# A of tile 0 behind the first weights on SyncE's queue, A of tile 1 on ScalarE's, the gathers' index made by VectorE

## The chip, the core and the metric

The kernel runs on one core of one Trainium2 chip. The metric is the device time of one execution in microseconds (us), as the median of several runs. Profiled executions come from the chip's profiler; all times inside them count from the start of the span.

The engines are TensorE (PE; its weight loads are listed apart as PEld), VectorE (DVE), ScalarE (ACT), GpSimd (POOL) and SyncE (SP, which here only issues DMAs). Each engine works through its own list of instructions in order and waits on semaphores where the program says so. ACT and POOL issue DMAs too, besides their arithmetic.

## What is computed

64 sequences of 32 rows and 512 columns pass through two residual layers. In each, a sequence picks its own weights by an index:

```python
def reference(x, itok_B_0_15, itok_B_0_23, L0_cond_weights, W, b, lora_As, lora_Bs):
    x = x + jnp.einsum('bct,bcd->bdt', x, L0_cond_weights[itok_B_0_15])
    base_out = jnp.einsum('bti,oi->bto', x, W) + b
    h = jnp.einsum('bti,bir->btr', x, lora_As[itok_B_0_23])
    lora_out = jnp.einsum('btr,bro->bto', h, lora_Bs[itok_B_0_23])
    return x + base_out + lora_out * 2.0
```

x is 64x32x512 in float32, W is 512x512, a lora_A is 512x16, a lora_B is 16x512.

## The kernel before

**Tiles.** Four sequences make one tile of 128 rows, so there are 16 tiles (u = 0 to 15). The two layers are swapped where that is possible: z = x (I + W) + x A B is made first, and the small mixing matrix of layer 0 is put on z afterwards (`mix`). For a tile the main product runs over four chunks k of 128 input columns. The host lays out x transposed.

**Precision.** Tiles 1 to 15 use split products: each operand is cut into a rounded part (ACT writes x_hi, wa) and a rest (DVE writes x_lo and the rest part of wa), and three fast products are summed (`products`, L548). The wide buffer wa holds W plus identity beside the A matrices. Tile 0 alone is computed in plain float32, straight from the loaded data: its main product is `first_chunk` (L619), its product with A is L626, its product with B is L580 (`lora(0, half)`).

**The start.** Host data for the start lie in one tensor `first`, which SP loads in five pieces (`load_first`, L209): piece 0 is half of x of tile 0 with W chunk 0, piece 1 the other half with W chunk 1, piece 2 is W chunk 2, piece 3 is W chunk 3, and piece 4 (`PIECE_OF_X1`) is x of tile 1. ACT first issues the two small loads of indices (L313, L314), then, after it has read four adapter numbers from the first of them, the four loads of A of tile 0 (L323, 32 KB each, 256 bytes to a partition). SP, after its five pieces, reads adapter numbers too and issues four loads of A of tile 1 (`load_a(1)`, L224), then x of tile 2 (L214), the weights of layer 0 (L237), A of tile 2 and so on.

**The steps around the change.** In program order:

- DVE adds the identity to the diagonal block of each W chunk (`add_identity`, L445) and makes the rest of each W chunk (`rest_w`, L449), then the two halves of the rest of x of tile 1 (`rest_x1`, L434), then the rests of A of tile 1 (`rest_a`, L455).
- ACT rounds W chunks 0 to 2 (`round_w`, L353), rounds the first half of x of tile 1 (`round_x1(0)`, L343), copies A of tile 0 into its place for the product (L388), rounds the second half of x of tile 1, A of tile 1 (L363) and W chunk 3.
- PE runs nine warm-up products on zeros (L541), `first_chunk` for k = 0 to 3, which needs piece k and for one half of its columns the added identity, then L626 with A of tile 0 (waits for `a0_ready`), then the main product of tile 1 (L548), whose first step waits for W chunk 0, for the first half of x of tile 1 and for the first half of A of tile 1, rests included. After four of its eight steps come the two halves of L580, which wait for the first gather of B and for the masked product of L626.
- POOL makes the identity and masks, then the row index for all gathers of B (L274, L276, from ids_p_sb), and then for each tile copies one column of the index (`gather_b`, L289) and issues an indirect DMA (L291). Three gathers are issued ahead.

Afterwards the loop over tiles 1 to 14 runs with loads three tiles ahead.

Of the kernel before, what the change touches and what calls it, by code (L numbers as in the profile page):

```python
# [10 lines left out]
ALU = mybir.AluOpType  # L11
# [5 lines left out]
def lora_residual_program(nc, first, xt, ids_row, ids_of_p, w0, bias, lora_a, lora_b, out):  # L17
# [5 lines left out]
    _, _, KC, _ = xt.shape  # L23
    O = out.shape[2]
    TILES = xt.shape[0] + 2
    C, S0, _ = w0.shape
    SLOTS, _, _, R = lora_a.shape
    T = KC * P
    J = P // C
# [6 lines left out]
    NA = 3  # L36
# [7 lines left out]
    PIECE_OF_X1 = 4  # L44
    DIAGONAL_HALF = tuple(k * P // HALF for k in range(KC))
    HJ = J // 2
# [12 lines left out]
    with ExitStack() as ctx:  # L59
# [143 lines left out]
        @block.sync  # L203
        def _(sp):
            adapters = [sp.alloc_register(f"adapter{j}") for j in range(J)]

            def load_first(n):
                at = slice(PIECES[n], PIECES[n + 1])
                sp.dma_start(first_sb[:, at], first[:, at]).then_inc(first_loaded[n], 16)  # L209

            def load_x(u):
                if u >= 2 + NX:
                    sp.wait_ge(x_ready, u - NX + 1)
                sp.dma_start(x_raw[(u - 2) % NX][:, :, :], xt[u - 2]).then_inc(x_loaded[(u - 2) % NX], 16)  # L214

            def load_a(u):
                if u == NA:
                    sp.wait_ge(a0_ready, 1)
                elif u > NA:
                    sp.wait_ge(a_ready, 2 * (u - NA))  # L220
                sp.load(adapters, ids_sb[0:1, u * J:(u + 1) * J])
                for j in range(J):
                    slot = sp.snap(adapters[j], min_val=0, max_val=SLOTS - 1)
                    sp.dma_start(a_raw[u % NA][:, j:j + 1, :, :].rearrange("p j k r -> p j (k r)"),  # L224
                                 lora_a[bass.ds(slot, 1)].rearrange("s p k r -> p s (k r)")
                                 ).then_inc(a1_half_loaded[j // HJ] if u == 1 else a_loaded[u % NA], 16)

            def store_y(u):
                sp.wait_ge(y_ready, u + 1)
                sp.dma_start(out_rows[u * P:(u + 1) * P, :], y_sb[u % 2][:, :]).then_inc(y_stored[u % 2], 16)  # L230

            for n in range(len(PIECES) - 1):
                load_first(n)
            sp.wait_ge(ids_loaded, 16)
            load_a(1)
            load_x(2)
            sp.dma_start(w0_raw[:, :, :], w0).then_inc(w0_loaded, 16)  # L237
            load_a(2)
            load_x(3)
            for u in range(1, TILES):  # L240
                if u + 2 < TILES:
                    load_a(u + 2)
                if u == 1:
                    sp.dma_start(bias_sb[:, :], bias).then_inc(bias_loaded, 16)
                    load_x(4)
                if u + 4 < TILES:
                    load_x(u + 4)
                if u >= 2:
                    store_y(u - 2)
            store_y(LAST - 1)  # L250
            for half in range(2):
                sp.wait_ge(y_ready, LAST + 1 + half)
                sp.dma_start(out_rows[LAST * P:(LAST + 1) * P, cols(half)],
                             y_sb[LAST % 2][:, cols(half)]).then_inc(y_stored[LAST % 2], 16)
            sp.wait_ge(y_stored[0], 16 * (TILES // 2))
            sp.wait_ge(y_stored[1], 16 * (TILES // 2 + 1))

        @block.gpsimd
        def _(pool):
            pool.memset(ident[:, :], 0.0).then_inc(ident_zero, 1)  # L260
            for s in range(2):
                pool.memset(m_raw[s][:, :], 0.0).then_inc(m_zero, 1)
            pool.wait_ge(ident_zero, 1)
            pool.affine_select(out=ident[:, :], in_=ident[:, :], compare_op=ALU.not_equal, fill=1.0,
                               base=0, pattern=[[-1, P]], channel_multiplier=1).then_inc(ident_ready, 1)
            pool.memset(own_mask0[:, :, :], SCALING).then_inc(mask0_step, 1)
            pool.wait_ge(mask0_step, 1)
            pool.affine_select(out=own_mask0[:, :, :], in_=own_mask0[:, :, :], compare_op=ALU.is_ge, fill=0.0,
                               base=0, pattern=[[-R, J], [0, C]], channel_multiplier=1).then_inc(mask0_step, 1)
            pool.wait_ge(mask0_step, 2)  # L270
            pool.affine_select(out=own_mask0[:, :, :], in_=own_mask0[:, :, :], compare_op=ALU.is_ge, fill=0.0,
                               base=R - 1, pattern=[[R, J], [0, C]], channel_multiplier=-1).then_inc(mask0_step, 1)
            pool.wait_ge(ids_p_loaded, 16)
            pool.tensor_copy(r_of_p[:, :], ids_p_sb[:, TILES:TILES + 1]).then_inc(r_ready, 1)  # L274
            pool.wait_ge(r_ready, 1)
            pool.tensor_scalar(b_index[:, :], ids_p_sb[:, 0:TILES], float(R), r_of_p[:, 0:1],  # L276
                               ALU.mult, ALU.add).then_inc(b_index_ready, 1)
            pool.wait_ge(b_index_ready, 1)

            def gather_b(u):  # L280
                s = u % NB
                if u >= NB:
                    pool.wait_ge(b_gathered[s], 16 * (u // NB))
                if u == NB:
                    pool.wait_ge(lora_done, 2)
                elif u > NB:
                    pool.wait_ge(b_ready, u - NB)
                rows = slice(0, JR if u == 0 else P)
                pool.tensor_copy(b_index_slot[s][:, :], b_index[:, u:u + 1]).then_inc(b_index_copied, 1)  # L289
                pool.wait_ge(b_index_copied, u + 1)  # L290
                pool.indirect_dma_start(  # L291
                    b_raw[s][rows, :], None, lora_b.rearrange("s r o -> (s r) o"),
                    bass.IndirectOffsetOnAxis(ap=b_index_slot[s][rows, 0:1], axis=0)).then_inc(b_gathered[s], 16)

            def split_m(u):
                s = u % 2
                pool.wait_ge(m_raw_ready, u + 1)
                if u >= 2:
                    pool.wait_ge(y_computed, u - 1)
                pool.tensor_copy(m_hi[s][:, :], m_raw[s][:, :]).then_inc(m_hi_ready, 1)  # L300
                pool.wait_ge(m_hi_ready, u + 1)
                pool.tensor_tensor(m_lo[s][:, :], m_raw[s][:, :], m_hi[s][:, :], ALU.subtract).then_inc(m_ready, 1)  # L302

            for u in range(NB):
                gather_b(u)
            for u in range(LAST):
                split_m(u)
                if u + NB < TILES:
                    gather_b(u + NB)

        @block.scalar
        def _(act):
# [2 lines left out]

            act.wait_ge(zeros_ready, 1)
            act.copy(scratch[:, :], zeros[:, 0:1])  # L317
            adapters0 = [act.alloc_register(f"adapter0_{j}") for j in range(J)]
            act.wait_ge(ids_loaded, 16)
            act.load(adapters0, ids_sb[0:1, 0:J])  # L320
            for j in range(J):
                slot = act.snap(adapters0[j], min_val=0, max_val=SLOTS - 1)
                act.dma_start(a_raw[0][:, j:j + 1, :, :].rearrange("p j k r -> p j (k r)"),  # L323
                              lora_a[bass.ds(slot, 1)].rearrange("s p k r -> p s (k r)")
                              ).then_inc(a_loaded[0], 16)

            conds = [act.alloc_register(f"cond{j}") for j in range(J)]

# [11 lines left out]
            def round_x1(half):  # L340
                if half == 0:
                    act.wait_ge(first_loaded[PIECE_OF_X1], 16)
                act.copy(x_hi[1][:, chunks(half), :], x_of(1)[:, chunks(half), :]).then_inc(x_hi_ready, 1)  # L343
# [33 lines left out]
            def round_z(u, half):  # L377
                act.wait_ge(lora_done, 2 * u + half + 1)
                if u >= 2:
# [3 lines left out]
            round_w(0)  # L383
            round_w(1)
            round_w(2)
            round_x1(0)
            act.wait_ge(a_loaded[0], 16 * J)
            act.copy(a0_sb[:, :, :].rearrange("p k (j r) -> p k j r", j=J),  # L388
                     a_raw[0][:, :, :, :].rearrange("p j k r -> p k j r")).then_inc(a0_ready, 1)
            round_x1(1)  # L390
            round_a(1)
            round_w(KC - 1)
# [30 lines left out]
        def _(dve):  # L423
# [18 lines left out]
            def add_identity(k):  # L442
                dve.wait_ge(first_loaded[k], 16)
                diagonal = w_raw(k)[:, k * P:(k + 1) * P]
                nc.vector.tensor_tensor(diagonal, diagonal, ident[:, :], ALU.add).then_inc(w_plus_i, 1)  # L445
# [37 lines left out]
            def finish_y(u):  # L483
                dve.wait_ge(y_computed, u + 1)
                if u >= 2:
                    dve.wait_ge(y_stored[u % 2], 16 * (u // 2))
                nc.vector.tensor_tensor(y_sb[u % 2][:, :], y_ps[u % 2][:, :], bias_sb[:, :],  # L487
                                        ALU.add).then_inc(y_ready, 1)

            dve.wait_ge(ident_ready, 1)  # L490
            add_identity(0)
            for k in range(KC - 1):
                add_identity(k + 1)
                rest_w(k)
            rest_x1(0)
# [221 lines left out]
```

## Time and profile before

| | us |
|---|---|
| median of 3 runs | 85.14 |
| lowest and highest of them | 84.99, 85.22 |
| the profiled execution | 85.35 |
| its span, first to last instruction | 83.6 |

| engine | busy, us | share of the span |
|---|---|---|
| PE | 79.6 | 95% |
| PEld | 71.8 | 86% |
| DVE | 59.3 | 71% |
| ACT | 52.0 | 62% |
| POOL | 35.0 | 42% |

A profiled execution's own time is 1.75 us longer than its span; that part lies outside the program's instructions. Busy times are sums over the whole span; they say which engine is fullest, and the waits near an engine's first instructions say where a start is late.

### The profile page before, as it was taken

To read this page: it belongs to the slowest core of one execution; us is meant where nothing else is said; L and a number is where in the kernel's file an instruction comes from. 1 tells how busy PE (TensorE), PEld (TensorE's weight loads), DVE (VectorE), ACT (ScalarE), POOL (GpSimd) and SP (SyncE) were. 2 spreads that over 40 slices of the span, in tenths; PEclk is the share of its full clock that TensorE was granted. 3 is DMA by queue.
4 is the path that set the end of the run, shared out by engine and by line. 5 is a ranking of instruction groups with operands and counts; after the bars stand their busy time and mean duration, and the time that the engine had idled before them with its cause. 6 is when DMAs were issued, how large, how long until landed. Compare 5 with 4: busy or idle time off the path is not lost.

```text
span 83.6 us, 1999 instructions
## 1 busy us (share of the span) xinstructions
PE 79.6 (95%) x521; PEld 71.8 (86%) x521; DVE 59.3 (71%) x154; ACT 52.0 (62%) x179; POOL 35.0 (42%) x75
## 2 busy tenths in 40 slices
PE   4999999999999999999999999999999999999970
PEld 2368688999899999999999999999999999999930
DVE  2048495885888787777878787888787777876540
ACT  1545757766566675958666666666685957669120
POOL 6128888844442617080715344342617080303000
PEclk9999999999999999999999999999999999999999
DMA  0999779899776768676586878676874734120333
GB/s 13 307 347 315 143 199 261 165 365 329 209 239 163 239 196 245 197 206 213 143 250 171 238 178 241 174 248 151 219 211 159 177 110 152 45 92 7 119 125 125
DMA packets 15997, 16.06 MB, mean 192 GB/s; under 512 B 10225, under 2 KB 10482, under 8 KB 15986
## 3 DMA queue, kind: packets, MB, share of 16 engines
q1 hardware_dynamic: 14016, 11.74, 47.4%
q0 software_dynamic: 1248, 4.06, 17.0%
q10 hardware_dynamic: 722, 0.14, 0.9%
q14 instruction: 7, 0.06, 0.3%
q8 instruction: 4, 0.07, 0.3%
HBM read 11.74 MB, written 4.19 MB: 191 GB/s over the span
## 4 chain that ended last, share of the span: by engine, by line
PE 85%; DMA 6%; ACTq 3%; ACT 2%; issue 1%; DVE 1%
PE z_ps L548 58%; PE z_ps L585 9%; DMA a_raw<-in_lora_a 6%; PE y_ps L596 4%; PE y_ps L600 4%; PE y_ps L598 4%; PE ht_ps L572 2%; ACTq L323 1%; PE z_ps L580 1%; PE ht_ps L626 1%; ACT L317 1%; PE y_last L608 1%; PE y_ps L608 1%; ACTq L313 1%; DVE y_sb L534 1%
## 5 line engine op out<-in xcount | busy, mean ns | idle before, releaser
L548 PE MATMUL z_ps<-wa,x_hi 128*128 128x288 f32 (+2 forms) x240 | 50.3, 301 | 0.0
L548 PEld LDWEIGHTS z_ps<-wa,x_hi 128*128 128x128 f32 x240 | 38.0, 188 | 1.8 <-issue 0.5
L548 PE MATMUL z_ps<-wa,x_lo 128*128 128x288 f32 (+2 forms) x120 | 35.5, 296 | 0.0
L548 PEld LDWEIGHTS z_ps<-wa,x_lo 128*128 128x128 f32 x120 | 22.6, 188 | 0.0
L291 POOL DMA_INDIRECT b_raw<-in_lora_b,b_index_slot x16 | 17.6, 1097 | 4.4 <-POOL b_index_slot L289 4.4
L300 POOL CAST m_hi<-m_raw 128x128 fp32r<-128x128 f32 x15 | 4.4, 293 | 31.5 <-ACT m_raw L337 31.5
L480 DVE TENSOR_TENSOR z_lo<-z_ps,z_hi 128x256 fp32r<-128x256 f32 x30 | 11.3, 420 | 6.4 <-ACT z_hi L381 6.4
L381 ACT CAST z_hi<-z_ps 128x256 fp32r<-128x256 f32 x30 | 9.7, 376 | 9.7 <-PE z_ps L585 9.6
L337 ACT COPY m_raw<-w_raw 32x32 f32 x64 | 13.8, 216 | 1.8 <-DVE w_raw L502 1.2
L439 DVE TENSOR_TENSOR x_lo<-x_raw,x_hi 128x512 fp32r<-128x512 f32 x14 | 9.7, 690 | 3.5 <-ACT x_hi L349 3.5
L460 DVE TENSOR_TENSOR b_lo<-b_raw,b_hi 128x512 fp32r<-128x512 f32 x15 | 10.4, 693 | 1.6 <-ACT b_hi L369 1.1
L487 DVE TENSOR_TENSOR y_sb<-y_ps,bias_sb 128x512 f32<-128x512 f32 x15 | 10.2, 683 | 0.9 <-PE y_ps L600 0.9
L369 ACT CAST b_hi<-b_raw 128x512 fp32r<-128x512 f32 x15 | 9.5, 633 | 0.7 <-DMA b_raw<-in_lora_b,b_index_slot 0.7
L349 ACT CAST x_hi<-x_raw 128x512 fp32r<-128x512 f32 x14 | 8.7, 622 | 0.0
L375 ACT CAST h_split<-z_ps 128x64 fp32r<-128x64 f32 x15 | 3.2, 212 | 8.5 <-PE z_ps L548 8.4
L585 PE MATMUL z_ps<-b_hi,ht_sb 128*128 128x256 f32 x30 | 8.1, 293 | 0.0
L585 PE MATMUL z_ps<-b_lo,ht_sb 128*128 128x256 f32 x30 | 7.8, 281 | 0.0
L363 ACT CAST wa<-a_raw 128x128 fp32r<-128x128 f32 x30 | 7.5, 299 | 0.0
L302 POOL TENSOR_TENSOR m_lo<-m_raw,m_hi 128x128 fp32r<-128x128 f32 x15 | 6.9, 461 | 1.2
L455 DVE TENSOR_TENSOR wa<-a_raw,wa 128x128 fp32r<-128x128 f32 x30 | 7.3, 284 | 0.0
L596 PE MATMUL y_ps<-z_hi,m_hi 128*128 128x512 f32 x15 | 6.0, 401 | 0.0
L600 PE MATMUL y_ps<-z_lo,m_hi 128*128 128x512 f32 x15 | 5.9, 395 | 0.0
(51 smaller groups left out, 78.8 us busy)
## 6 DMA issues: line engine op xcount, KB each, us to landing
out<-y_sb SPq DMA_DIRECT2D x15, 256.0 KB, 2.4
x_raw<-in_xt SPq DMA_DIRECT2D x14, 256.0 KB, 2.9
a_raw<-in_lora_a SPq DMA_DIRECT2D x60, 32.0 KB
first_sb<-in_first SPq DMA_DIRECT2D x2, 384.0 KB, 4.0
first_sb<-in_first SPq DMA_DIRECT2D x3, 256.0 KB, 4.8
b_raw<-in_lora_b,b_index_slot POOLq DMA_INDIRECT x16, 4.0
bias_sb<-in_bias SPq DMA_DIRECT2D x1, 256.0 KB, 5.2
out<-y_sb SPq DMA_DIRECT2D x2, 128.0 KB, 1.7
```

What stands on the lines that cost most here:

```text
L291: pool.indirect_dma_start(b_raw[s][rows, :], None, lora_b.rearrange("s r o -> (s r) o"), bass.IndirectOffsetOnAxis(ap=b_index_slot[s][rows ...
L337: last = act.copy(m_raw[s][q, q], w0_raw[:, bass.ds(slots[j], 1), :])
L369: act.copy(b_hi[u % 2][:, :], b_raw[u % NB][:, :]).then_inc(b_hi_ready, 1)
L381: act.copy(z_hi[u % 2][:, cols(half)], z_of(u, half)).then_inc(z_hi_ready, 1)
L439: nc.vector.tensor_tensor(x_lo[u % 2][:, :, :], x_of(u), x_hi[u % 2][:, :, :], ALU.subtract).then_inc(x_ready, 1)
L460: nc.vector.tensor_tensor(b_lo[u % 2][:, :], b_raw[u % NB][:, :], b_hi[u % 2][:, :], ALU.subtract).then_inc(b_ready, 1)
L480: nc.vector.tensor_tensor(z_lo[u % 2][:, cols(half)], z_of(u, half), z_hi[u % 2][:, cols(half)], ALU.subtract).then_inc(z_ready, 1)
L487: nc.vector.tensor_tensor(y_sb[u % 2][:, :], y_ps[u % 2][:, :], bias_sb[:, :], ALU.add).then_inc(y_ready, 1)
L548: done = nc.tensor.matmul(target, (x_lo if lo_x else x_hi)[s][:, k, :], moving(lo_w), start=first and not lo_x and not lo_w, stop=last and ...
L585: last = nc.tensor.matmul(z_of(u, half), ht_sb[u % 2][:, :], b_part[u % 2][:, cols(half)], start=False, stop=True, skip_group_check=True)
L596: nc.tensor.matmul(y_ps[s][:, :], m_hi[s][:, :], z_hi[s][:, :], start=True, stop=False, skip_group_check=True)
L600: nc.tensor.matmul(y_ps[s][:, :], m_hi[s][:, :], z_lo[s][:, :], start=False, stop=True, skip_group_check=True).then_inc(y_computed, 1)
```

## The change

Four DMA issues change place with four others, one load is issued later on SP, two small operations go from POOL to DVE, and two ACT steps swap.

- SP: after pieces 0 to 3 it waits for the adapter numbers and issues the four loads of A of tile 0. Only then comes piece 4 (x of tile 1). A of tile 1 is gone from this queue.
- ACT: its four early loads are now A of tile 1, in halves. Its copy of A of tile 0 now stands ahead of both halves of x of tile 1.
- POOL no longer makes the index; DVE does, between the second `add_identity` and the first `rest_w`.

```diff
-            for n in range(len(PIECES) - 1):
+            for n in range(PIECE_OF_X1):
                 load_first(n)
             sp.wait_ge(ids_loaded, 16)
-            load_a(1)
+            load_a(0)
+            load_first(PIECE_OF_X1)
             load_x(2)
...
-            pool.wait_ge(ids_p_loaded, 16)
-            pool.tensor_copy(r_of_p[:, :], ids_p_sb[:, TILES:TILES + 1]).then_inc(r_ready, 1)
-            pool.wait_ge(r_ready, 1)
-            pool.tensor_scalar(b_index[:, :], ids_p_sb[:, 0:TILES], float(R), r_of_p[:, 0:1],
-                               ALU.mult, ALU.add).then_inc(b_index_ready, 1)
             pool.wait_ge(b_index_ready, 1)
...
-            act.load(adapters0, ids_sb[0:1, 0:J])
+            act.load(adapters1, ids_sb[0:1, J:2 * J])
             for j in range(J):
-                slot = act.snap(adapters0[j], min_val=0, max_val=SLOTS - 1)
-                act.dma_start(a_raw[0][:, j:j + 1, :, :].rearrange("p j k r -> p j (k r)"),
+                slot = act.snap(adapters1[j], min_val=0, max_val=SLOTS - 1)
+                act.dma_start(a_raw[1][:, j:j + 1, :, :].rearrange("p j k r -> p j (k r)"),
                               lora_a[bass.ds(slot, 1)].rearrange("s p k r -> p s (k r)")
-                              ).then_inc(a_loaded[0], 16)
+                              ).then_inc(a1_half_loaded[j // HJ], 16)
...
-            round_x1(0)
             act.wait_ge(a_loaded[0], 16 * J)
             act.copy(a0_sb[:, :, :].rearrange("p k (j r) -> p k j r", j=J),
                      a_raw[0][:, :, :, :].rearrange("p j k r -> p k j r")).then_inc(a0_ready, 1)
+            round_x1(0)
             round_x1(1)
...
+            def index_b():
+                dve.wait_ge(ids_p_loaded, 16)
+                nc.vector.tensor_copy(r_of_p[:, :], ids_p_sb[:, TILES:TILES + 1]).then_inc(r_ready, 1)
+                dve.wait_ge(r_ready, 1)
+                nc.vector.tensor_scalar(b_index[:, :], ids_p_sb[:, 0:TILES], float(R), r_of_p[:, 0:1],
+                                        ALU.mult, ALU.add).then_inc(b_index_ready, 1)
...
             add_identity(0)
-            for k in range(KC - 1):
+            add_identity(1)
+            index_b()
+            rest_w(0)
+            for k in range(1, KC - 1):
                 add_identity(k + 1)
                 rest_w(k)
```

On SP, from the first load to x of tile 2 (x_raw0), before; a_raw1 is A of tile 1, and the 128x512 pieces are pieces 2, 3 and 4:

```order
L209 DMA first_sb<-in_first 128x768 x2
L209 DMA first_sb<-in_first 128x512 x3
L221 TENSOR_LOAD ids_sb [waits ids_loaded]
L223 ISA
L224 DMA a_raw1<-in_lora_a 128x64
...
L214 DMA x_raw0<-in_xt 128x512
```

and now:

```order
L209 DMA first_sb<-in_first 128x768 x2
L209 DMA first_sb<-in_first 128x512 x2
L221 TENSOR_LOAD ids_sb [waits ids_loaded]
L223 ISA
L224 DMA a_raw0<-in_lora_a 128x64
...
L209 DMA first_sb<-in_first 128x512
L214 DMA x_raw0<-in_xt 128x512
```

Piece 4 moved behind the register load and four small DMAs, which now fetch A of tile 0; x of tile 2 has as many instructions ahead of it as before.

On ACT, after its DMA issues, before:

```order
L353 CAST wa<-first_sb 128x2x256 [waits w_plus_i] x3
L343 CAST x_hi1<-first_sb 128x256 [waits first_loaded4]
L388 COPY a0_sb<-a_raw0 128x256 [waits a_loaded0]
L343 CAST x_hi1<-first_sb 128x256
L363 CAST wa<-a_raw1 128x4x32 [waits a1_half_loaded0]
```

and now:

```order
L350 CAST wa<-first_sb 128x2x256 [waits w_plus_i] x3
L384 COPY a0_sb<-a_raw0 128x256 [waits a_loaded0]
L340 CAST x_hi1<-first_sb 128x256 [waits first_loaded4]
L340 CAST x_hi1<-first_sb 128x256
L360 CAST wa<-a_raw1 128x4x32 [waits a1_half_loaded0]
```

The copy of A of tile 0 moved ahead of both halves of x of tile 1.

On DVE, at the second piece of the weights, before:

```order
L445 TENSOR_TENSOR first_sb<-first_sb,ident 128x128 [waits first_loaded1]
L449 TENSOR_TENSOR wa<-first_sb,wa 128x2x256 [waits w_hi_ready]
L445 TENSOR_TENSOR first_sb<-first_sb,ident 128x128 [waits first_loaded2]
```

and now:

```order
L442 TENSOR_TENSOR first_sb<-first_sb,ident 128x128 [waits first_loaded1]
L489 CAST r_of_p<-ids_p_sb 128x1 [waits ids_p_loaded]
L491 TENSOR_SCALAR b_index<-ids_p_sb,r_of_p 128x16 [waits r_ready]
L446 TENSOR_TENSOR wa<-first_sb,wa 128x2x256 [waits w_hi_ready]
L442 TENSOR_TENSOR first_sb<-first_sb,ident 128x128 [waits first_loaded2]
```

Two small operations and a wait for the second load of indices came in between.

## Rows read from the trace of the kernel before

**Rows 1.** The page: busy time; the chain that ended last, by engine.
```profile
PE 79.6 (95%) x521; PEld 71.8 (86%) x521; DVE 59.3 (71%) x154; ACT 52.0 (62%) x179; POOL 35.0 (42%) x75
...
PE 85%; DMA 6%; ACTq 3%; ACT 2%; issue 1%; DVE 1%
```

**Rows 2.** Timeline of weight loads: start us, us, what, count, [idle before, releaser].
```profile
4.59 4.42 PEld L619 LDWEIGHTS z_ps<-first_sb 128*128 128x128 f32 x16 [0.41 <-DMA first_sb<-in_first]
...
7.74 0.19 PEld L619 LDWEIGHTS z_ps<-first_sb 128*128 128x128 f32 x1
...
8.82 0.19 PEld L619 LDWEIGHTS z_ps<-first_sb 128*128 128x128 f32 x1
...
9.59 0.85 PEld L626 LDWEIGHTS ht_ps<-first_sb,a_sb 128*64 128x64 f32 x8 [0.59 <-ACT a_sb L388]
10.61 0.30 PEld L548 LDWEIGHTS z_ps<-wa,x_hi 128*128 128x128 f32 x2 [0.17 <-issue]
...
12.49 0.73 PEld L580 LDWEIGHTS z_ps<-b_raw,ht_sb 64*128 64x128 f32 x4 [0.26 <-issue]
13.54 0.30 PEld L548 LDWEIGHTS z_ps<-wa,x_hi 128*128 128x128 f32 x2 [0.33 <-issue]
```

**Rows 3.** Timeline of ACT, 6 to 10 us.
```profile
6.72 0.62 ACT L353 CAST wa<-first_sb 128x512 fp32r<-128x512 f32 x1 [0.19 <-DVE first_sb L445]
8.17 0.40 ACT L343 CAST x_hi<-first_sb 128x256 fp32r<-128x256 f32 x1 [0.84 <-DMA first_sb<-in_first]
9.14 0.40 ACT L388 COPY a_sb<-a_raw 128x256 f32<-128x256 f32 x1 [0.56 <-DMA a_raw<-in_lora_a]
9.45 0.40 ACT L343 CAST x_hi<-first_sb 128x256 fp32r<-128x256 f32 x1
```

**Rows 4.** Timeline of DVE, 0 to 11 us.
```profile
0.89 0.11 DVE L424 MEMSET zeros<- 128x64 uint32 x1 [0.89 <-PEq L707]
...
5.80 0.69 DVE L449 TENSOR_TENSOR wa<-first_sb,wa 128x512 fp32r<-128x512 f32 x1
6.40 0.28 DVE L445 TENSOR_TENSOR first_sb<-first_sb,ident 128x128 f32<-128x128 f32 x1
...
10.22 0.49 DVE L455 TENSOR_TENSOR wa<-a_raw,wa 128x128 fp32r<-128x128 f32 x2
```

**Rows 5.** Timeline of the queues of SP and ACT: issues of DMAs.
```profile
0.81 2.30 SPq L209 DMA_DIRECT2D first_sb<-in_first  x5
...
2.74 0.36 ACTq L323 DMA_DIRECT2D a_raw<-in_lora_a  x1
...
3.87 1.93 SPq L224 DMA_DIRECT2D a_raw<-in_lora_a  x4
5.85 0.42 SPq L214 DMA_DIRECT2D x_raw<-in_xt  x1
```

**Rows 6.** Line L214 (x), the loads issued up to 20 us: issue to landing.
```profile
DMA to landing us min/median/max: 3.6/4.3/5.7
```

**Rows 7.** Tile x_raw over the whole span: issue to landing.
```profile
DMA to landing us min/median/max: 2.6/2.9/5.7
```

**Rows 8.** Line L291, the first gather alone: issue to landing.
```profile
DMA to landing us min/median/max: 3.9/3.9/3.9
```

**Rows 9.** Windows: us, PE, PEld, DVE, ACT, POOL busy, clock, DMA share, GB/s.
```profile
0.00:8.00 8.00, 6.94 (x20) 4.02 (x21) 3.29 (x13) 3.33 (x5) 3.76 (x14) 1.00 0.79 242
8.00:9.00 1.00, 1.00 (x6) 0.90 (x5) 0.48 (x2) 0.40 (x1) 0.70 (x2) 1.00 0.88 265
...
10.00:11.00 1.00, 1.00 (x10) 0.83 (x9) 0.91 (x4) 1.00 (x4) 0.97 (x1) 1.00 0.70 83
```

**Rows 10.** Timeline of POOL, 5 to 10 us.
```profile
5.79 0.74 POOL L274 CAST r_of_p<-ids_p_sb 128x1 f32<-128x1 int32 x1 [3.28 <-DMA ids_p_sb<-in_ids_of_p]
6.64 0.91 POOL L276 TENSOR_SCALAR b_index<-ids_p_sb,r_of_p 128x16 uint32<-128x16 int32 x1
7.62 0.52 POOL L289 COPY b_index_slot<-b_index 128x1 uint32<-128x1 uint32 x1
8.44 1.10 POOL L291 DMA_INDIRECT b_raw<-in_lora_b,b_index_slot  x1 [0.30 <-POOL b_index_slot L289]
9.56 0.19 POOL L289 COPY b_index_slot<-b_index 128x1 uint32<-128x1 uint32 x1
```

More of the change, by code:

```diff
@@ L225, in load_a @@
                                  lora_a[bass.ds(slot, 1)].rearrange("s p k r -> p s (k r)")
-                                 ).then_inc(a1_half_loaded[j // HJ] if u == 1 else a_loaded[u % NA], 16)
+                                 ).then_inc(a_loaded[u % NA], 16)
             def store_y(u):
@@ L317, in _ @@
             act.copy(scratch[:, :], zeros[:, 0:1])
-            adapters0 = [act.alloc_register(f"adapter0_{j}") for j in range(J)]
+            adapters1 = [act.alloc_register(f"adapter1_{j}") for j in range(J)]
             act.wait_ge(ids_loaded, 16)
-            act.load(adapters0, ids_sb[0:1, 0:J])
+            act.load(adapters1, ids_sb[0:1, J:2 * J])
             for j in range(J):
-                slot = act.snap(adapters0[j], min_val=0, max_val=SLOTS - 1)
-                act.dma_start(a_raw[0][:, j:j + 1, :, :].rearrange("p j k r -> p j (k r)"),
+                slot = act.snap(adapters1[j], min_val=0, max_val=SLOTS - 1)
+                act.dma_start(a_raw[1][:, j:j + 1, :, :].rearrange("p j k r -> p j (k r)"),
                               lora_a[bass.ds(slot, 1)].rearrange("s p k r -> p s (k r)")
-                              ).then_inc(a_loaded[0], 16)
+                              ).then_inc(a1_half_loaded[j // HJ], 16)
             conds = [act.alloc_register(f"cond{j}") for j in range(J)]
```

## Prediction

> **What bounds the kernel now.** I read the page first: PE is busy 95% of the span, and 85% of the chain that ended last is PE's [rows 1]. In the loop over tiles PE follows its own list without a gap, so its length stays, and a change at the start counts only by how much it moves the moment at which PE enters that list for good. Second view: PE's weight loads near the start [rows 2], where an idle time before a group shows a late input. Tile 0's main product runs from 4.59 and its last weight load starts at 8.82. The product with A of tile 0 (L626) starts at 9.59, after 0.59 idle that the copy of A on ACT ended. Tile 1's first product (L548) starts at 10.61; I call this moment T. Two short gaps of 0.26 and 0.33 follow around tile 0's product with B (12.49, 13.54). From there on there is nothing to win by this change.
>
> Third view: why T is 10.61. On ACT, A of tile 0 lands and is copied at 9.14, and the second half of x of tile 1 is rounded at 9.45 [rows 3]; its rest on DVE and then the rest of A of tile 1 follow at 10.22 [rows 4]; PE starts 0.39 later. x of tile 1 itself was there at 8.17 [rows 3]. So T hangs by two ways on the landing of A of tile 0 (9.12, just before its copy): through L626 and, since the copy stands ahead of the second half of x on ACT, through x.
>
> **The change part by part.**
>
> *A of tile 0 on SP, and ahead of x on ACT.* On ACT the order is now: copy of A of tile 0, first and second half of x, A of tile 1. Let L be the landing of x of tile 1. The first half starts at L + 0.02, the second 0.31 later (9.14 to 9.45 is one such copy), and from the second half's start to T it takes 10.61 - 9.45 = 1.16 [rows 2, 3]. So T = L + 1.49, if x comes last. From A of tile 0, landing at M, PE starts L626 at M + 0.47 and L548 1.02 later, so T = M + 1.49 too. PE's own floor: its last weight load of the main product is at 8.82 and such loads follow each other by about 0.21 (7.74 to 8.60 is four of them), so L626 could start at 9.03, and T is 9.03 + 1.02 = 10.05 at the earliest [rows 2]. The most this part can give is 0.56 us, for L and M of 8.56 or less. Break-even is a landing at 9.12.
>
> *When does x of tile 1 land now?* Before, SP issued five pieces from 0.81 in 2.30 us, some 0.46 each, and its first A load at 3.87, 0.76 after the last piece [rows 5]. Now four pieces end at about 2.63, the A loads start at 3.39 and take 1.93, and piece 4 is issued at about 5.35, where it was at 2.67 before. Its landing was at 8.15, which is 5.5 after its issue, so it was held by the data ahead of it and not by its issue. Two ways to bound L. By rows of the same load (x, 256 KB): 2.6 at least [rows 7], 3.6, 4.3 and 5.7 as least, median and most of those issued up to 20 us [rows 6]. That gives 7.95, 8.95, 9.65 and 11.05. By bytes: what must have moved is 1.57 MB of pieces, 0.26 MB of A of tiles 0 and 1 and some 0.14 MB of small things, 1.97 MB. The trace moved 242 GB/s x 8 us = 1.94 MB up to 8.0 and 265 GB/s then [rows 9], so it is 8.1, and data landed later than that: by the same account x of tile 1 before was due at 7.3 to 7.7 and landed at 8.15, so 0.45 to 0.85 later. That gives 8.6 to 9.0. I take **L = 9.2**, 3.85 after the issue, nearest to the row of 3.6: above the bytes' figure, since x now follows 256-byte rows on its own queue, and such rows were slow to land (the last A load on ACT was issued by 4.7 and the four landed by 9.12), and below the median of 4.3, since most of the loads in that median were issued later, with gathers beside them. T is then 10.69, which is **+0.08**. The bounds are L = 8.6 (-0.56 with the floor) and 9.65 (+0.53).
>
> *M.* A of tile 0 now stands behind piece 3, which landed at about 7.0, and ahead of x, so M lies between 7.0 and L; I take 8.5. It ends ahead of PE's 9.03 - 0.47 = 8.56. The wait of 0.59 at L626 goes, and what is late next is x.
>
> A page of the Trainium skill speaks against this move: "DMA: Bandwidth & Descriptors", section Queues, rings and completion order, says that a transfer's semaphore write comes only after all earlier writes of the same DMA engine, across its queues. By it L could not come before A of tile 1, now on ACT's queue, which would take over A of tile 0's 9.12, and T would be 10.61 or more: no gain is then to be had.
>
> *A of tile 1 on ACT.* Issued from 2.74 instead of 3.87 [rows 5], in the place of A of tile 0, so it lands by about 9.1. It is used at L + 0.64 on ACT, so it is hidden for any L above 8.5; it costs nothing.
>
> *The index on DVE.* Removed from POOL: 0.74 + 0.91 [rows 10]. Added to DVE: two operations on 1 and 16 columns. No such row exists on DVE; the shortest on it is 0.11 [rows 4], the same work on POOL took 1.65 in all. I take 0.3 for both with the hand-over between them, near the DVE row, with bounds of 0.2 and 1.65. It lies ahead of `rest_w(0)` at 5.80, so W chunk 2 gets its identity at 6.7 + 0.28 instead of 6.40 + 0.28 [rows 4]. PE wants that at 7.74 [rows 2], so 0.7 of cover is left; chunk 3 is wanted at 8.60 and has as much. Should the index take 1.65, chunk 2 would come at 8.3 and PE would stand 0.6 ahead of it; that would still end ahead of T, since PE waits for x about that long anyway. Cost: nothing. The second load of indices lands at 5.76 or so, ahead of 5.88, when DVE asks for it.
>
> *The gathers come earlier.* The index is ready at about 6.2 instead of 7.55. POOL's first copy (0.52), the step to the DMA (0.30) and the landing 3.9 after it [rows 8, 10] give 11.0 instead of 12.34. The gap of 0.26 at L580 [rows 2] is partly this landing; but the two other changes from split to plain products or back (10.61 with 0.17, 13.54 with 0.33) have such a gap with no gather. So I credit 0.05, between 0 and 0.15. If T were much earlier, the old landing would have eaten the gain, and the new one doesn't.
>
> The slot copy took 0.52 at 7.62 with DVE at work and 0.19 at 9.56 without [rows 10]. The Trainium skill ("SBUF — State Buffer", section Who interferes with whom) says why: a DVE operation with two inputs in SBUF and a GpSimd operation that reads SBUF block each other, the first one through. By it the first slot copy now waits for `rest_w(0)` to end, and the first gather would land at 11.3 rather than 11.0, still ahead of its use at 12.5: the sum stays.
>
> *Sum:* +0.08 - 0.05 = +0.03 us. The profiled span would be 83.6, its own time 85.4; the median of the runs is 0.2 below the profiled execution, and I go by the median: 85.14 + 0.03 = **85.17 us**.
>
> **Rivals.**
>
> *1. Faster: x lands early.* For: the bytes' figure says 8.6 to 9.0, and the wait for A of tile 0 goes for certain. Against: x is issued 2.7 later than before. With L = 8.7, T is 10.19: 0.42 + 0.05 saved, **84.67**. It decides below L = 8.9.
>
> *2. Slower: x becomes the late input.* Place: ACT's first copy of x of tile 1, behind which the second half, A of tile 1 and so PE stand. With the median of [rows 6], L = 9.65, T is 11.14: 0.53 - 0.05, **85.62**. It decides above L = 9.42. By the page named first, this rival gets stronger; the trace shows A landing 0.97 after x though x was issued only just before it, which agrees with slow 256-byte rows but not with that rule alone.
>
> *3. Slower: the early gather meets x.* Between 10 and 11 us the DMA engines were 70% busy and moved 83 GB/s [rows 9], when the first gather's data were due: they were held up. That stretch now comes at about 8.7 to 9.7. If it holds x for its 0.7, T is 11.4 and the time **85.85**. Against: x has moved its data by then by the bytes' figure.
>
> *4. The change does nothing:* the index is off the path in any case, and the two waits exchange places exactly. That is my forecast's own case, not apart from it. That PE's longer wait ahead of T (0.7 instead of the 0.59 and 0.17) lowers its clock is possible; the granted clock stayed at 1.00, which is 2.4 GHz, over the waits before [rows 9], so I give it no more than 0.02.
>
> **How the numbers follow.** Within 0.3% means within 0.25 us, about what a measurement of this kernel can tell from no change; that is L between about 8.9 and 9.42. Forecast 0.46; rival 1 0.27; rival 2 0.18; rival 3 0.07; the clock 0.02. So faster 0.27, same 0.46, slower 0.27. The range reaches from L = 8.63 (-0.5 with the gather, 84.6) to the time of rival 3 (85.8), and leaves out the floor's 84.5 and below, and loads as slow as 5.7.
>
> **What would show it.** On ACT, the copy of A of tile 0 ahead of x and the first half of x idle until a DMA at 9.0 to 9.4; L626 close behind the main product (9.0 to 9.2); L548's first weight load at 10.5 to 10.9 with an idle time of 0.5 or more ahead; DVE's two index operations at 5.9 with 0.1 each; the first gather issued at 7.0 or so. The end of the span moves as T does. I am wrong if x lands before 8.9 or after 9.45, if piece 2's or 3's identity makes the main product of tile 0 stand, or if a gap appears behind 14 us that was not there.

## The result: 85.68 us, 0.4% slower, and the profile after

| | before | after |
|---|---|---|
| median of 12 runs, us | 85.18 | 85.68 |
| ratio after to before, 95% interval | | 1.0045 [1.0024, 1.0067] |
| profiled execution, us | 85.35 | 85.68 |
| its span, us | 83.6 | 83.9 |
| T, tile 1's first product, us | 10.61 | 11.09 |

The ratio stands for 0.38 us (0.20 to 0.57). Runs at a lower granted clock (two of the twelve of after, 87.4 and 87.5 us at 0.98, none of before) are left out of the ratios here and below, but not of the medians. The forecast was 85.17 within 84.6 to 85.8: the time lies in the range, on the side that rival 2 named.

The page after, busy time and the chain that ended last, against [rows 1]: PE is as full as before, DVE has two more operations and POOL two fewer.

```profile
PE 79.5 (95%) x521; PEld 71.9 (86%) x521; DVE 59.6 (71%) x156; ACT 52.1 (62%) x179; POOL 32.4 (39%) x73
...
PE 95%; issue 1%; DVE 1%
```

The timeline of weight loads after, against [rows 2] (start us, us, what, count, idle before and its releaser):

```profile
8.62 0.41 PEld L626 LDWEIGHTS z_ps<-first_sb 128*128 128x128 f32 x2
9.36 0.85 PEld L633 LDWEIGHTS ht_ps<-first_sb,a_sb 128*64 128x64 f32 x8 [0.33 <-issue]
11.09 0.30 PEld L555 LDWEIGHTS z_ps<-wa,x_hi 128*128 128x128 f32 x2 [0.88 <-issue]
...
12.88 0.73 PEld L587 LDWEIGHTS z_ps<-b_raw,ht_sb 64*128 64x128 f32 x4 [0.16 <-issue]
13.93 0.30 PEld L555 LDWEIGHTS z_ps<-wa,x_hi 128*128 128x128 f32 x2 [0.33 <-issue]
```

The product with A of tile 0 (now L633) starts 0.23 earlier than before, at 9.36 instead of 9.59. But T is 11.09 and not 10.61: 0.88 of idle has come ahead of tile 1. "issue" there means that the profile shows no wait; which wait it is, ACT and DVE tell.

The timeline of ACT after, against [rows 3]:

```profile
8.46 0.41 ACT L384 COPY a_sb<-a_raw 128x256 f32<-128x256 f32 x1 [0.94 <-DMA a_raw<-in_lora_a]
9.61 0.71 ACT L340 CAST x_hi<-first_sb 128x256 fp32r<-128x256 f32 x2 [0.74 <-DMA first_sb<-in_first]
10.23 0.49 ACT L360 CAST wa<-a_raw 128x128 fp32r<-128x128 f32 x2
```

A of tile 0 landed at 8.44 (9.12 before), x of tile 1 at 9.59 (8.15 before). The two changed places: ACT had only to wait for x after it, A of tile 1 followed without a wait, and from the landing of x to T it is 11.09 - 9.59 = 1.50.

The timeline of DVE after, at the index and at the rest of x:

```profile
5.65 0.15 DVE L489 CAST r_of_p<-ids_p_sb 128x1 f32<-128x1 int32 x1
5.83 0.23 DVE L491 TENSOR_SCALAR b_index<-ids_p_sb,r_of_p 128x16 uint32<-128x16 int32 x1
5.98 0.69 DVE L446 TENSOR_TENSOR wa<-first_sb,wa 128x512 fp32r<-128x512 f32 x1
...
10.05 0.77 DVE L431 TENSOR_TENSOR x_lo<-first_sb,x_hi 128x256 fp32r<-128x256 f32 x2 [1.78 <-issue]
```

POOL and SP after, against [rows 10] and [rows 5]: the slot copy and the first gather, and the issues of A of tile 0 and of x of tile 1.

```profile
6.13 0.57 POOL L285 COPY b_index_slot<-b_index 128x1 uint32<-128x1 uint32 x1 [3.61 <-DVE b_index L491]
7.00 1.42 POOL L287 DMA_INDIRECT b_raw<-in_lora_b,b_index_slot  x1 [0.29 <-POOL b_index_slot L285]
...
3.39 1.93 SPq L224 DMA_DIRECT2D a_raw<-in_lora_a  x4
5.37 0.43 SPq L209 DMA_DIRECT2D first_sb<-in_first  x1
```

x of tile 1 was issued at 5.37 and landed at 9.59: 4.2 us.

### The profile page after: what moved, and what is told of

It reads as the page before. It is cut to its first block, busy times and chain, and to the rows that moved or that the text cites. A ratio compares the mean times of both kernels' runs of the same rounds, so it can differ in the third digit from the quotient of the medians.

```text
span 83.9 us, 1999 instructions
## 1 busy us (share of the span) xinstructions
PE 79.5 (95%) x521; PEld 71.9 (86%) x521; DVE 59.6 (71%) x156; ACT 52.1 (62%) x179; POOL 32.4 (39%) x73
## 4 chain that ended last, share of the span: by engine, by line
PE 95%; issue 1%; DVE 1%
PE z_ps L555 58%; PE z_ps L592 9%; PE z_ps L626 5%; PE ht_ps L548 5%; PE y_ps L603 4%; PE y_ps L607 4%; PE y_ps L605 4%; PE ht_ps L579 2%; PE z_ps L587 1%; PE ht_ps L633 1%; PE y_last L615 1%; PE y_ps L615 1%; DVE y_sb L541 1%; DVE zeros L421 0%
## 5 line engine op out<-in xcount | busy, mean ns | idle before, releaser
L287 POOL DMA_INDIRECT b_raw<-in_lora_b,b_index_slot x16 | 16.8, 1047 | 4.4 <-POOL b_index_slot L285 4.1
```

What stands on the lines that cost most here:

```text
L287: pool.indirect_dma_start(b_raw[s][rows, :], None, lora_b.rearrange("s r o -> (s r) o"), bass.IndirectOffsetOnAxis(ap=b_index_slot[s][rows ...
```

## The experiments

Four questions: is it the loads or the index; is the late x due to the early gather or to what stands ahead of it on its queue; what do the changed orders of SP and of ACT each cost; and can the loads be ordered so that both A of tile 0 and x come early. Ratios are to the kernel before, run beside each group on the same chip; a single execution has no ratio. T is read from each kernel's timeline of weight loads.

### The index alone, and the loads alone

The index alone is the kernel before with this (the DVE part as in the change):

```diff
-            pool.wait_ge(ids_p_loaded, 16)
-            pool.tensor_copy(r_of_p[:, :], ...
...
+            add_identity(1)
+            index_b()
+            rest_w(0)
```

> The kernel before with the index of the gathers made by VectorE and nothing else changed. Theory (the loads cost, the index gives): the third gather no longer lands late, so ScalarE's wait of 0.70 us for B of tile 2 (before at 19.45) is gone, and the gaps ahead of L580, of tile 1's and of tile 2's product with B shrink by 0.1, 0.06 and 0.12 as they did in the changed kernel; the start (first product of tile 1 at 10.61) stays. Time 0.2 to 0.3 us below before. Rival (the index is off the path, what the changed kernel won back came from the later start alone): time as before within 0.1 us.

Measured: 85.10 us, ratio 0.9985 [0.9961, 1.0009]. Its profiled execution had a span of 83.1 and T at 10.19, which looks like a gain of half a microsecond. The reason is a row of ACT that the index doesn't touch:

```profile
8.72 0.40 ACT L383 COPY a_sb<-a_raw 128x256 f32<-128x256 f32 x1 [0.58 <-DMA a_raw<-in_lora_a]
```

A of tile 0 landed 0.42 earlier than in before's execution. Whether that came with the index or by chance, a repeat on another chip had to show:

> The kernel before with only the index made by VectorE, measured again because the first interval (0.9961 to 1.0009) holds no change. Theory (the third gather's late landing costs ScalarE 0.7 and TensorE 0.1 to 0.2): ratio 0.997 to 0.999. Rival (off the path): 1.000.

Measured: 85.49 us, ratio 1.0018 [0.9987, 1.0049]; in its profile the same copy starts at 9.52 and T is 11.02.

```profile
9.52 0.40 ACT L383 COPY a_sb<-a_raw 128x256 f32<-128x256 f32 x1 [0.68 <-DMA a_raw<-in_lora_a]
```

So the index on DVE makes no difference that can be measured (both intervals hold 1 and end at 1.0049 at most), and the landing of A of tile 0 on ACT's queue scatters by 0.8 between executions.

The loads alone are the changed kernel with the index back on POOL, so that the first gather is issued at 8.19 and not at 7.00.

```diff
-            index_b()
...
+            pool.wait_ge(ids_p_loaded, 16)
+            pool.tensor_copy(r_of_p[:, :], ...
```

> The changed kernel with the index back on GpSimd: the DMA issues and ScalarE's order are changed, the index is not. Theory A (x of tile 1 is late because it is issued 2.7 us later and finds the queue run dry): x still lands at 9.4 to 9.6, the first product of tile 1 starts at about 11.0, and the time is 0.5 to 0.6 us above before, that is 0.2 above the changed kernel. Rival B (the early gather holds x up: in the changed kernel the gather's rows began at 9.0 and x landed at 9.6): x lands at 9.1 or earlier, the first product of tile 1 starts at 10.6, and the time is as before or faster than the changed kernel.

Measured: 85.75 us, ratio 1.0055 [1.0034, 1.0076]. ACT and the weight loads of it:

```profile
9.64 0.71 ACT L345 CAST x_hi<-first_sb 128x256 fp32r<-128x256 f32 x2 [0.76 <-DMA first_sb<-in_first]
...
8.93 0.85 PEld L628 LDWEIGHTS ht_ps<-first_sb,a_sb 128*64 128x64 f32 x8 [0.63 <-ACT a_sb L389]
11.19 0.30 PEld L550 LDWEIGHTS z_ps<-wa,x_hi 128*128 128x128 f32 x2 [1.41 <-DVE x_lo L436]
```

The whole loss comes with the loads and ACT's new order, which this kernel keeps together. x lands as late (9.62) with the gather issued 1.2 us later, so rival 3, the early gather that holds x up, falls. Here the profile also names the wait ahead of T: the rest of x.

### Undoing the place of x

The changed kernel, with x of tile 1 back in front of A of tile 0 on SP:

```diff
-            for n in range(PIECE_OF_X1):
+            for n in range(len(PIECES) - 1):
...
             load_a(0)
-            load_first(PIECE_OF_X1)
```

> The changed kernel with piece 4 (x of tile 1) issued right behind piece 3 again, ahead of A of tile 0 on SyncE's queue; A of tile 1 stays on ScalarE's queue, the copy of A of tile 0 stays ahead of x on ScalarE, the index stays on VectorE. Theory (each 256 KB ahead of a load costs it 0.75 to 1.1 us): x lands at about 8.2, A of tile 0 at 9.2 to 9.7, where A of tile 1 was in the kernel before, and is copied then; the first product of tile 1 starts 1.49 later, at 10.7 to 11.2, so the time is 0 to 0.4 above before. Rival (small loads on SyncE's queue land early, as A of tile 0 did in the changed kernel at 8.4, and x alone was late): A of tile 0 lands by 8.9 also behind x, the first product of tile 1 starts at 10.4, and the time is 0.4 us below before.

Measured: 86.31 us, ratio 1.0099 [1.0068, 1.0129].

```profile
9.87 0.40 ACT L383 COPY a_sb<-a_raw 128x256 f32<-128x256 f32 x1 [2.43 <-DMA a_raw<-in_lora_a]
10.18 0.70 ACT L339 CAST x_hi<-first_sb 128x256 fp32r<-128x256 f32 x2
```

x had landed before ACT came to it, and now A of tile 0 is the late one, at 9.85, 1.4 later than in the changed kernel. Behind its copy both halves of x still have to be rounded, and T is 11.64. In these two orders, whichever stands second on SP's queue is late.

A middle way, with x between the second and the third load of A of tile 0:

```diff
                 for j in range(J):
+                    if u == 0 and j == 2:
+                        load_first(PIECE_OF_X1)
...
-            load_first(PIECE_OF_X1)
```

> The changed kernel with piece 4 (x of tile 1) between the second and third of the four loads of A of tile 0 on SyncE's queue, so issued at about 4.4 instead of 5.37. Theory (in the changed kernel x is bound by its own issue, 4.2 us from issue to landing): x lands about 1 us earlier, at 8.6, and A of tile 0 at 8.9 or later. Rival (x is bound by the data ahead of it, two small loads less are worth at most half of the 1.5 us): x lands at 8.9 to 9.1.

Measured in one execution: 85.69 us, span 84.0, T 11.02.

```profile
9.25 0.41 ACT L385 COPY a_sb<-a_raw 128x256 f32<-128x256 f32 x1 [1.92 <-DMA a_raw<-in_lora_a]
9.56 0.71 ACT L341 CAST x_hi<-first_sb 128x256 fp32r<-128x256 f32 x2
```

A of tile 0 lost 0.8 and x, which doesn't wait any more, starts only 0.05 earlier. When x landed this trace doesn't show, since ACT came to it only behind the copy, so it doesn't decide between the two expectations. T is that of after's repeat within 0.02.

### ACT's order alone

The kernel before with only the swap on ACT:

```diff
-            round_x1(0)
             act.wait_ge(a_loaded[0], 16 * J)
             act.copy(a0_sb[:, :, :]...
+            round_x1(0)
```

> The kernel before with ScalarE's copy of A of tile 0 ahead of the first half of x of tile 1, nothing else changed. Theory (the start hangs on ScalarE's order behind the landing of A of tile 0 at 9.12): one more copy of 0.31 us stands between the landing and the rest of A of tile 1, so the first product of tile 1 starts at 10.92 instead of 10.61, and the time is 0.3 us above before. Rival (TensorE's own product with A of tile 0 and the change of product type set 10.61, ScalarE's order has room): time as before within 0.1 us.

Measured: 85.57 us, ratio 1.0039 [1.0022, 1.0056].

```profile
8.75 0.40 ACT L387 COPY a_sb<-a_raw 128x256 f32<-128x256 f32 x1 [1.61 <-DMA a_raw<-in_lora_a]
9.06 0.71 ACT L343 CAST x_hi<-first_sb 128x256 fp32r<-128x256 f32 x2
...
10.61 0.30 PEld L548 LDWEIGHTS z_ps<-wa,x_hi 128*128 128x128 f32 x2 [0.56 <-DVE x_lo L434]
```

From the copy to T it is 10.61 - 8.75 = 1.86; before it was 10.61 - 9.14 = 1.47 [rows 2, 3]. The first half of x (0.31) no longer lies in the idle time ahead of the copy. The profiled execution hides this 0.39, since A of tile 0 landed early in it; the runs show it (+0.33). So where A of tile 0 is last, the swap costs about as much as the whole change lost. In the changed kernel x is last and the swap is free: the copy is done 0.7 before x lands.

### Both kernels once more, and x issued late with nothing but pieces ahead

For the spread of T, the two kernels unchanged:

> The kernel before, unchanged, profiled a second time. In two of the kernels measured so far, whose early loads are those of before, A of tile 0 was copied at 8.72 and 8.75, not at 9.14. Theory (the trace of before showed a late landing; the usual one is 8.7): the copy stands at 8.6 to 8.8 and the first product of tile 1 starts at 10.1 to 10.3. Rival (9.14 is usual for before): copy at 9.1, first product at 10.6.

> The changed kernel, profiled a second time. Theory (x of tile 1 lands late by its place in the queue): ScalarE's first rounding of x of tile 1 starts at 9.4 to 9.8 again and the first product of tile 1 at 10.9 to 11.3. Rival (it was a chance of one execution): 9.0 to 9.2 and 10.6.

Measured: before 85.34, span 83.6, T 10.71; after 85.70, span 84.0, T 11.04. One more execution of the kernel before, run beside these, took 85.92, so single times say little here. ACT of before, then of after:

```profile
9.22 0.40 ACT L388 COPY a_sb<-a_raw 128x256 f32<-128x256 f32 x1 [0.81 <-DMA a_raw<-in_lora_a]
```

```profile
9.57 0.71 ACT L340 CAST x_hi<-first_sb 128x256 fp32r<-128x256 f32 x2 [0.76 <-DMA first_sb<-in_first]
```

So 9.1 to 9.2 was no exception for before, and the late x of after came again. The two profiles of before and the two of the index alone have a mean T of 10.63; the two of after and the one of the loads alone 11.11.

The third asks what made x take 4.2 us. It is the kernel before, but SP waits for the second load of indices before it issues x of tile 1, so that x goes out at 5.5, as in the changed kernel, while only pieces 0 to 3 stand ahead of it on SP. A of tile 0 stays on ACT's queue, and A of tile 1 follows x.

```diff
-            for n in range(len(PIECES) - 1):
+            for n in range(PIECE_OF_X1):
                 load_first(n)
+            sp.wait_ge(ids_p_loaded, 16)
+            load_first(PIECE_OF_X1)
```

> The kernel before, with SyncE waiting for the second load of indices (about 5.6) ahead of piece 4, so x of tile 1 is issued at 5.6 to 5.7 with nothing but pieces 0 to 3 ahead of it on its queue; A of tile 0 stays on ScalarE's queue, A of tile 1 comes after x and is later by as much. Only the landing of x is looked at. Theory (a load issued that late needs about 4 us by itself): x lands at 9.3 to 9.8. Rival (the 512 rows of 256 bytes ahead of x on its own queue made it late): without them x needs 2.6 to 2.9 us, as the median load of x does, and lands at 8.3 to 8.6.

The run was made for the landing of x, since every later load of SP is late too. Line L209 in the stretch of that one issue, and ACT:

```profile
DMA to landing us min/median/max: 2.8/2.8/2.8
```

```profile
8.33 0.40 ACT L345 CAST x_hi<-first_sb 128x256 fp32r<-128x256 f32 x1 [1.25 <-DMA first_sb<-in_first]
```

x needs 2.8 from its issue, not 4.2: it lands at 8.3, 1.3 earlier than in the changed kernel, though issued 0.1 later. So the late issue alone doesn't make 4.2; what stands around x does. Three things differ here at once, and the runs don't part them: four loads of A on x's own queue ahead of it, the number of A loads that are out before x (four instead of eight), and what follows on its queue. In the changed kernel x of tile 2 (256 KB) and the weights of layer 0 were issued at 5.85 and 6.32, here only at 8.56 and 9.04, when x had landed. That the 256-byte rows ahead are the cause is thus argued and not shown. The windows of the changed kernel agree with it (us, PE, PEld, DVE, ACT, POOL busy, clock, DMA share, GB/s):

```profile
6.00:7.00 1.00, 1.00 (x4) 0.82 (x3) 1.00 (x4) 0.49 (x2) 0.58 (x2) 1.00 1.23 268
7.00:8.00 1.00, 1.00 (x7) 0.87 (x6) 1.00 (x3) 0.52 (x1) 1.00 (x1) 1.00 0.93 179
8.00:9.00 1.00, 1.00 (x6) 0.90 (x5) 0.27 (x1) 0.41 (x1) 0.71 (x3) 1.00 0.88 319
```

From 7 to 8 us the DMA engines are 93% busy and move 179 GB/s, while from 8 to 9, when x comes, a share of 0.88 moves 319. The late-x kernel, with four loads of A in place of eight, has such a stretch too, one microsecond earlier:

```profile
6.00:7.00 1.00, 1.00 (x7) 0.87 (x6) 1.00 (x4) 0.81 (x2) 0.89 (x2) 1.00 0.91 183
```

The same trace shows something that was not asked for. Here is the last of the four loads of A of tile 0 (line L325, issued at 4.3 on ACT's queue as in the kernel before), then ACT's copy of it and T:

```profile
DMA to landing us min/median/max: 3.1/3.1/3.1
...
8.64 0.40 ACT L390 COPY a_sb<-a_raw 128x256 f32<-128x256 f32 x1
10.11 0.30 PEld L550 LDWEIGHTS z_ps<-wa,x_hi 128*128 128x128 f32 x2 [0.17 <-issue]
```

A of tile 0 landed at 7.4, where it took until 8.7 to 9.5 in the traces with x and A of tile 1 issued early beside it, and with x at 8.3 both inputs were early at once. T is 10.11, 0.5 earlier than before, although ACT copied A only behind the first half of x. So the landing of A seems to depend on what else SP has issued; one trace shows it. The price came later: the whole kernel took 88.69 us, for a reason that stands in the last section. A kernel that holds back x less, or keeps A of tile 2 in time, was not run.

### x of tile 2 ahead of A of tile 1

If small rows delay what follows, A of tile 0 on ACT's queue might land earlier with fewer small rows beside it. The kernel before with this, and the same with the index on DVE:

```diff
-            load_a(1)
             load_x(2)
+            load_a(1)
```

> The kernel before with x of tile 2 issued ahead of A of tile 1 on SyncE's queue, nothing else changed. It asks whether the landing of A of tile 0 (8.7 to 9.5 in the traces with its loads on ScalarE's queue), on which the start hangs, suffers from the 256-byte rows of A of tile 1 beside it. Theory (it does: small rows on both queues at once slow each other): A of tile 0 is copied by 8.6 and the first product of tile 1 starts at 10.0 to 10.2, if A of tile 1 still lands by 9.3; time 0.3 us below before. Rival (bytes count, not rows): A of tile 0 as before, A of tile 1 0.5 to 0.8 later, at 9.6 to 10.0, so the first product of tile 1 starts at 10.6 to 11.0 and the time is 0.1 to 0.4 above before.

> The same with the index made by VectorE as well. Theory (the index is off the path): the time of the kernel with x of tile 2 first, within 0.1 us. Rival (earlier gathers collide with A of tile 1, which now lands later): 0.2 us or more above it.

Measured: 85.92 us, ratio 1.0061 [1.0028, 1.0093], and 85.87 us, ratio 1.0071 [1.0037, 1.0104]; the two are alike within 0.1, so the index is off the path here too. ACT of the first, then the copy in the second:

```profile
8.71 0.40 ACT L343 CAST x_hi<-first_sb 128x256 fp32r<-128x256 f32 x1 [1.61 <-DMA first_sb<-in_first]
9.95 0.40 ACT L388 COPY a_sb<-a_raw 128x256 f32<-128x256 f32 x1 [0.84 <-DMA a_raw<-in_lora_a]
...
9.31 0.40 ACT L383 COPY a_sb<-a_raw 128x256 f32<-128x256 f32 x1 [1.03 <-DMA a_raw<-in_lora_a]
```

In the first, A of tile 0 lands later, at 9.93, and so does x of tile 1, at 8.69; in the second, A's 9.29 lies within what the kernels with the old order showed. The expectation (A by 8.6, time 0.3 below) falls by both times, which are 0.5 and 0.6 above before: by the times, 256 KB of x of tile 2 beside A of tile 0 are no better than the 128 KB of A of tile 1 in small rows. None of the kernels that ran beats the kernel before in time.

## Why the prediction was right or wrong

**T decides the time.** Right, and more exactly than it was put. Span less T, from the profiled executions:

| kernel | T | span | span - T |
|---|---|---|---|
| before | 10.61 | 83.6 | 73.0 |
| before again | 10.71 | 83.6 | 72.9 |
| after | 11.09 | 83.9 | 72.8 |
| after again | 11.04 | 84.0 | 73.0 |
| index alone, twice | 10.19, 11.02 | 83.1, 83.8 | 72.9, 72.8 |
| loads alone | 11.19 | 84.1 | 72.9 |
| x first | 11.64 | 84.5 | 72.9 |
| copy first | 10.61 | 83.4 | 72.8 |
| x between | 11.02 | 84.0 | 73.0 |
| x of tile 2 first, without and with the index | 11.43, 10.79 | 84.4, 83.8 | 73.0, 73.0 |

Behind T all of them take 72.8 to 73.0, with spans known to 0.1. "From there on there is nothing to win" holds, and what is lost ahead of T is not made up beyond this scatter. The late-x run stands apart; the last section has it.

**T = L + 1.49.** Right: 1.50 in after, 1.49 in its repeat (9.55 to 11.04), 1.57 with the loads alone. The mechanism of the forecast, A of tile 0 and x exchanging places as the last input, is what happened.

**T = M + 1.49.** Wrong for the new order on ACT, though it didn't decide. The 1.49 was read where only the second half of x stood behind the copy of A; now both halves do. From A's landing to T it is 1.88 with the copy first and 1.79 with x first and x between. So a landing of A breaks even at about 8.8, not 9.12, and the full gain of 0.56 would have wanted M of about 8.2.

**L = 9.2, 3.85 after the issue.** This is the term that was mis-sized. It measured 4.2, and L 9.59, 0.39 more; with it T is 0.48 later instead of 0.08, which covers the 0.38 (0.20 to 0.57) of the runs. By its own sign, "I am wrong if x lands before 8.9 or after 9.45", the prediction was wrong on L; the time fell within 84.6 to 85.8 only because that range was drawn to reach the time of rival 3. The choice fell between the bytes' figure and the median of [rows 6], near the low end of the latter, since "most of the loads in that median were issued later". The late-x run shows that x issued as late can be faster still (2.8), and that what stood around it in the changed kernel cost 1.4; how much of it the rows of A ahead of it made is open. The text had named them ("x now follows 256-byte rows on its own queue") and given them no price: above the 8.6 to 9.0 by bytes it added 0.2 to 0.6. That small rows might cost more was in the trace: the last 32 KB of A of tile 0 landed 4.8 after their issue (4.3 to 9.12).

**M = 8.5.** Right: 8.44, 8.39 in the repeat, 8.46 with the loads alone. Three executions lie within 0.07, where the old place gave 8.7 to 9.5. A of tile 1 on ACT's queue was "about 9.1" in the forecast and landed at 8.1 with the loads alone; it was hidden either way.

**PE's floor of 9.03 for the product with A.** Too low. L633 started at 9.36 with its A long there (its copy began at 8.46), and 0.33 ahead of it are put down to issue. The same 0.33 stands at 13.54 before [rows 2] and at 13.93 after. The prediction saw such a gap at each change between plain and split products, but left it out between the plain main product and the one with A. With it the floor of T is 9.36 + 1.02 = 10.38, so the most that the change could have brought was about 0.2 and not 0.56: rival 1 at 84.67 was out of reach in this execution. With the loads alone L628 started at 8.93, behind its own copy, since PE had gone through tile 0 sooner; there the floor is 9.95.

**The index costs nothing.** Right: 0.15 and 0.23 on DVE, the second overlapping the first `rest_w`, and two ratios, for the index alone, whose intervals hold 1.

**The gather brings 0.05.** The gap at the product with B went from 0.26 to 0.16. But it is 0.16 too with the copy first or the loads alone, with the index on POOL, and 0.17 in the repeat of before, where T is 10.71. In the profile of before the first gather was issued at 8.44 and landed 3.9 later, at 12.3 to 12.4, just ahead of its use at 12.49, so the 0.10 may be its lateness in that one execution; with the copy first, at the same T of 10.61, it was issued at 8.27, took 3.3 and left 0.16. So the 0.10 can't be put down to the index.

**The slot copy waits for DVE.** It took 0.57 at 6.13 and ended at 6.70, with `rest_w(0)` ending at 6.67. The Trainium skill ("SBUF — State Buffer", section Who interferes with whom) says that a DVE operation with two inputs in SBUF and a GpSimd operation that reads SBUF block each other: the trace agrees, 0.57 here and 0.19 for the same copy alone [rows 10].

**The page against the move.** The rule cited in the prediction (x's semaphore not before A of tile 1) was given the price of A landing at 9.12. With the loads alone, the last load of A of tile 1 was issued on ACT's queue at 4.3 (line L325):

```profile
DMA to landing us min/median/max: 3.8/3.8/3.8
```

So A of tile 1 had landed at 8.1, and x landed at 9.62, 1.5 later. The order of landings agrees with the rule, but A of tile 1 didn't hold x until 9.6, and the rule left room for an L well below 9.12. It doesn't explain the 1.4.

**The chances.** Rival 2 stated what happened (L 9.65, T 11.14, 85.62; measured 9.59, 11.09, 85.68) and had 0.18, less than the faster one with 0.27. Both unknown prices on the way of x, four issues of small rows ahead and A of tile 1 ahead on the other queue, point to a later landing, and only the bytes' figure spoke for an earlier one. That the slower side should have had the larger share is a judgement after the fact.

## What to carry to other kernels

When two inputs are wanted at about the same time, putting one ahead of the other on a queue may only exchange who is late, as it did here: work out both landings in the new order, with all that is issued beside and behind them, and price loads in small rows by the time such loads took in the trace, not by their bytes alone. The one run in which both were early held other loads back, and paid for it a tile later. A moment that all later work hangs on (here T) is worth finding first, since span less that moment was the same within about 0.3 us in twelve executions, and nearly every experiment can be read from one row. When one profiled execution shows a gain or loss of half a microsecond, look whether an input that the edit doesn't touch landed at another time before crediting the edit.

## What the hardware showed that was not expected

**Behind a short stand of PE its clock fell.** In the late-x run A of tile 2 was late (ACT waited 2.27 for it) and PE stood for 2.29 ahead of tile 2:

```profile
17.16 0.30 PEld L550 LDWEIGHTS z_ps<-wa,x_hi 128*128 128x128 f32 x2 [2.29 <-issue]
```

Its windows from 18 us (clock is the third column from the right):

```profile
18.00:19.00 1.00, 1.00 (x7) 0.72 (x5) 0.91 (x3) 0.94 (x5) 0.64 (x1) 0.77 0.97 350
19.00:20.00 1.00, 1.00 (x6) 1.00 (x5) 0.64 (x2) 0.00 (x0) 0.87 (x3) 0.50 0.65 150
...
21.00:22.00 1.00, 1.00 (x6) 1.00 (x6) 0.37 (x1) 0.72 (x3) 0.26 (x1) 0.52 1.00 370
22.00:23.00 1.00, 1.00 (x10) 1.00 (x9) 0.90 (x3) 0.54 (x2) 0.00 (x0) 1.00 0.82 220
```

The granted clock fell from 1.00 (2.4 GHz) to 0.50 (1.2 GHz) only after PE was at work again, for some 3.4 us, and span less T is 76.9 there instead of 72.9, 4.0 more. The idle time is 2.3 of it; by an estimate from the windows at half clock (26 matmuls in the four from 18 to 22 us, where before has 38) PE fell a further 1.1 to 1.4 behind. The waits of 0.9 to 2.0 ahead of T in the other profiled executions have no such fall behind them: with x first, where PE stood for 1.98 and again for 0.47, span less T is as always. That the stand caused the fall is argued from this one execution.

**Small rows land irregularly.** A of tile 0 on ACT's queue, issued at the same times within 0.1 us, landed at 8.70 (index alone), 8.73 (copy first), 9.12 and 9.20 (before) and 9.50 (index again), and at 7.4 in the late-x run, where SP issued nothing behind pieces 0 to 3 until 5.5.

**Two small operations on DVE take 0.38, on POOL 1.65** [rows 10]. On POOL they ran beside DVE's work on the weights, as the slot copy did; how much of the 1.65 that made is not shown.
